# A third PSUM bank for row maxima, a respaced schedule and packed narrow products in a fused two-layer attention kernel

## The reference

```python
x = x + L0_xattn(layernorm(x), ctx)      # 16 heads of width 16, q and k normalised per head
x = x + L0_ffn(layernorm(x))             # P = x@U1 (256 -> 64), H = gelu(P@V1 + b1) (64 -> 1024),
                                         # Q = H@U2 (1024 -> 64), Q@V2 + b2 (64 -> 256)
x = x + L1_xattn(layernorm(x), ctx, mask)# one head of width 16: q = x@Wq+bq, k = c@Wk+bk, v = c@Wv+bv;
                                         # scores normalised over the keys (mean, std), softmax, @v,
                                         # the head tiled 16 times, @Wout + bout
x = x + L1_ffn(layernorm(x))             # soft mixture: logits x@phi, softmax over the batch (dispatch)
                                         # and over the slots (combine), 64 experts of 32 slots
```

## Time and profile before

| | before |
|---|---|
| median of three runs | 6526.37 us |
| the profiled execution's own time | 6520.53 us |
| its span | 6518.7 us |
| PE busy | 5927.6 us, 91% |
| DVE busy | 3677.9 us, 56% |
| ACT busy | 3300.6 us, 51% |
| POOL busy | 2407.3 us, 37% |

### The profile page before, as it was taken

One profiled execution on the slowest core, in us unless ns is written; L12 is line 12 of the kernel. 1 busy time (PEld: TensorE's weight loads), 2 busy tenths in 40 slices (PEclk: granted clock), 3 DMA queues, 4 the chain that ended last, 5 costly groups with the idle time before them and its releaser, 6 DMA issues. The chain is left out here.

```text
span 6518.7 us, 93097 instructions
## 1 busy us (share of the span) xinstructions
PE 5927.6 (91%) x35613; PEld 2981.1 (46%) x35613; DVE 3677.9 (56%) x6989; ACT 3300.6 (51%) x6257; POOL 2407.3 (37%) x2686
## 2 busy tenths in 40 slices
PE   3789999999999999999999999997599999998999
PEld 1223333333333333333333333322388888886888
DVE  3565656656566565565665656661366666652333
ACT  1366666666666666666666666654222222223332
POOL 3226355363462634636346364443222222220000
PEclk9799999999999999999999999997799999999999
DMA  2441432414324143241332423310356666666553
GB/s 63 78 76 51 79 72 58 83 50 77 69 58 85 49 76 69 61 86 50 74 70 60 84 56 71 62 28 15 127 187 214 221 213 214 209 211 249 211 195 117
DMA packets 417819, 680.30 MB, mean 104 GB/s; under 512 B 61376, under 2 KB 316432, under 8 KB 415072
## 3 DMA queue, kind: packets, MB, share of 16 engines
q1 hardware_dynamic: 307552, 565.29, 34.0%
q10 hardware_dynamic: 109824, 109.07, 5.0%
HBM read 455.04 MB, written 218.39 MB: 103 GB/s over the span
## 5 line engine op out<-in xcount | busy, mean ns | idle before, releaser
L1193 DVE TENSOR_REDUCE mx<-psum 128x1 f32<-128x401 f32 x4096 | 2212.1, 570 | 1612.8 <-PE psum L767 1603.7
L1038 ACT ACTIVATE probs<-psum 128x512 f32<-128x512 f32 (+1 forms) x3328 | 1910.5, 599 | 906.6 <-PE psum L789 903.5
L767 PE MATMUL psum<-kst,qst 96*128 96x401 bf16 x4096 | 1354.9, 343 | 191.9 <-DVE mx L1193 150.9
L789 PE MATMUL psum<-qst,kst 99*128 99x512 bf16 (+1 forms) x3328 | 1284.5, 386 | 49.8 <-ACT probs L1038 44.8
L800 PE MATMUL psum<-probs,vaug 128*17 128x512 f32 x6656 | 885.8, 604 | 0.0
L789 PEld LDWEIGHTS psum<-qst,kst 99*128 99x128 bf16 (+1 forms) x3328 | 328.8, 99 | 1177.1 <-ACT probs L1038 750.4
L767 PEld LDWEIGHTS psum<-kst,qst 96*128 96x128 bf16 x4096 | 402.6, 98 | 961.4 <-DVE mx L1193 756.1
L1486 POOL TENSOR_TENSOR disp<-disp,rz 128x2048 f32<-128x2048 f32 x64 | 294.3, 4599 | 925.4 <-DVE rz L1716 925.4
L1505 PE MATMUL psum<-phi,xT 128*128 128x128 f32 x4096 | 512.2, 280 | 39.2 <-DMA xT<-xnT_scratch 31.9
L1520 PE MATMUL psum<-disp,xnb 128*128 128x128 f32 x4096 | 495.5, 280 | 49.9 <-DMA xnb<-xn_scratch 30.7
L1505 PEld LDWEIGHTS psum<-phi,xT 128*128 128x128 f32 x4096 | 480.4, 193 | 86.9 <-issue 79.2
(11 more groups left out here) (190 smaller groups left out, 7527.2 us busy)
## 6 DMA issues: line engine op xcount, KB each, us to landing
xnb<-xn_scratch SPq DMA_DIRECT2D x256, 512.0 KB, 3.8
kst<-k_planes SPq DMA_DIRECT2D x384, 200.1 KB, 8.7
logit_scratch<-disp ACTq DMA_DIRECT2D x64, 1024.0 KB, 5.3
xT<-logit_scratch SPq DMA_DIRECT2D x32, 2048.0 KB, 8.3
k_planes<-pl SPq DMA_DIRECT2D x96, 384.0 KB, 3.2
y_scratch<-ysb ACTq DMA_DIRECT2D x128, 256.0 KB, 5.3
vaug<-v_scratch SPq DMA_DIRECT2D x64, 442.0 KB, 4.3
v_scratch<-vst SPq DMA_DIRECT2D x48, 544.0 KB, 3.1
```

Source lines behind the costliest of these rows:

```text
L767: mm(to[:, 0:PW], qst[g][0:NP, j, t * P:(t + 1) * P], kst[g][0:NP, j, k0:k0 + PW], start=True, stop=True).then_inc(m_full, 1)
L789: mm(bank[S_BANK[n % 2]][0:m, :], kst[g][0:NR, j, c * P:c * P + m], qst[g][0:NR, j, :], start=True, stop=True).then_inc(s_full, 1)
L1038: fn(probs[0:m, 4 * (k % 2) + j, :], bank[S_BANK[j % 2]][0:m, :], ACT.Exp, scale=float(HD) ** 0.5).then_inc(s_exp, 1)
L1193: v.tensor_reduce(mx[:, n % 2, u // 4, u % 4:u % 4 + 1], bank[M_BANK[r % 2]][:, 0:PW], AX.X, ALU.max).then_inc(m_free, 1)
```

## The change

Four things change together.

1. The ring for pieces gets a third bank, number 7, in 43 of the 52 steps (`LENT`: all but steps 38 to 46). The ring is now a list of homes: each use takes the bank that has been free for longest.
2. The tail, which had banks 6 and 7, keeps bank 6 alone except in steps 38 to 46, where `pv1` and `out` use bank 7. What alternated between the two now waits for its predecessor's copy; `V1` 4 to 7 go to the head's bank 5.
3. The pieces of a step stand elsewhere: the second comes behind the second score product, the third behind place 1, the fourth behind place 2, and the last behind `weigh_values`. The positions of nearly all tail entries are new.
4. Narrow products are packed in the array. `kv1` is cut into four lots of 128 tokens, each into its own 32 partitions of the bank; `U2` takes two chunks at once, into partitions 0 to 63 and 64 to 127, and `v2` sums the halves by a doubled weight; `s1` takes two chunks of keys at once, one on array rows 0 to 63 and one on rows 64 to 127, into banks 5 and 6. For this the layer 1 keys and queries are kept twice in SBUF, and the mean of the keys needs one small product (`km` on PE, `sel`).

Pieces of the diff that the prediction speaks of:

```diff
-        put((11.0, 11.34, 11.67, 12.0, 15.9, 16.67, 17.67, 18.67)[f], -1, "V1", f)
+        put((11.34, 12.0, 12.67, 13.34, 16.67, 17.67, 18.36, 20.0)[f], -1, "V1", f)
...
-        put(35.0 + 0.5 * c, -1, "s1", c)
+    for p in range((KC + 1) // 2):
+        put((36.0, 37.0, 38.34, 39.34, 40.67, 41.67, 43.0)[p], -1, "s1", p)
...
+LENT = [s < 38 or s > 46 for s in range(STEPS)]
...
+    last = {2: None, 3: None, 7: None}
+    ring, homes, back = {}, [], {}
+    for i, (use, k) in enumerate(order):
+        free = [m for m in (2, 3, 7) if m != 7 or (LENT[k % STEPS] and k < B * STEPS)]
+        home = min(free, key=lambda m: -1 if last[m] is None else last[m])
+        homes.append((home, last[home]))
...
                 for k in range(2):
-                    last = mm(hb[0:2 * A1, 0:m], w1kv[:, k, :], cT[:, n % 2, k, 0:m], start=(k == 0), stop=(k == 1))
+                    for j in range(-(-m // P)):
+                        w = min(P, m - j * P)
+                        last = mm(hb[32 * j:32 * j + 32, 0:w], w1kv[:, k, :], cT[:, n % 2, k, j * P:j * P + w],
+                                  start=(k == 0), stop=(k == 1), skip_group_check=True)
...
             def ring_bank(use):
-                n = RING[use]
-                if n >= 2:
-                    pe.wait_ge(m_free, n - 1)
-                return bank[M_BANK[n % 2]]
+                home = HOMES[RING[use]]
+                if home[1] is not None:
+                    pe.wait_ge(m_free, home[1] + 1)
+                if len(home) == 3 and home[2] >= 0:
+                    pe.wait_ge(t_dve, at("t_dve", home[2], "res", 3, QT - 1))
+                return bank[home[0]]
...
             def ffn_up(b, f):
-                before = ("u1",) if f < 2 else ("V1", f - 2) if f < 5 else ("V1", f - 1)
-                pe.wait_ge(t_act, at("t_act", b, *before))
-                to = b7 if f in (1, 3) else b6
-                mm(to[:, :], v1[:, f * P:(f + 1) * P], pT[0:RANK, :], start=True, stop=True).then_inc(t_mm, 1)
+                if f < 4:
+                    pe.wait_ge(t_act, at("t_act", b, *(("V1", f - 1) if f else ("u1",))))
+                    to, signal = b6, t_mm
+                else:
+                    head_bank(b, "V1", f)
+                    to, signal = hb, h_full
+                mm(to, v1[:, f * P:(f + 1) * P], pT[0:RANK, :], start=True, stop=True).then_inc(signal, 1)
...
+            def ffn_down(b, p):
+                if p == 0:
                     pe.wait_ge(t_act, at("t_act", b, "V1", 3))
-                pe.wait_ge(g_post, at("g_post", b, "gpost", f))
-                mm(b7[0:RANK, :], u2[:, f, :], hx[:, f % 4, :], start=(f == 0), stop=(f == FC - 1)).then_inc(t_mm, 1)
+                pe.wait_ge(g_post, at("g_post", b, "gpost", 2 * p + 1))
+                for a in range(2):
+                    last = mm(b6[RANK * a:RANK * a + RANK, :], u2[:, 2 * p + a, :], hx[:, (2 * p + a) % 4, :],
+                              start=(p == 0), stop=(p == FC // 2 - 1), skip_group_check=True)
+                last.then_inc(t_mm, 1)
...
+            def layer_one_scores(b, p):
+                head_bank(b, "s1", p)
+                if p >= 1:
+                    pe.wait_ge(t_act, at("t_act", b, "s1", p - 1))
                 else:
                     pe.wait_ge(t_dve, at("t_dve", b, "q1a"))
-                mm(to[0:m, :], kv1T[:, c * P:c * P + m], q1a, start=True, stop=True).then_inc(signal, 1)
+                c, m = 2 * p, key_rows(2 * p)
+                mm(hb[0:m, :], kv1T[0:64, c * P:c * P + m], q1a[0:64, :], start=True, stop=True).then_inc(h_full, 1)
+                if c + 1 < KC:
+                    mm(b6[:, :], kv1T[64:P, (c + 1) * P:(c + 2) * P], q1a[64:P, :], start=True,
+                       stop=True).then_inc(t_mm, 1)
...
                     woven_steps(b, steps, s, 0)
-                    piece()
                     score_columns(b, g, c, 1)
                     piece()
                     woven_steps(b, steps, s, 1)
+                    piece()
                     score_columns(b, g, c, 2)
+                    woven_steps(b, steps, s, 2)
                     piece()
-                    woven_steps(b, steps, s, 2)
                     score_columns(b, g, c, 3)
-                    piece()
```

More of the change, by code:

```diff
@@ new lines, in woven @@
+        put((12.68, 13.35, 14.01, 14.68, 18.35, 19.35, 20.35, 21.35)[f], -1, "gpost", f)
+    for p in range(FC // 2):
+        put((16.34, 18.34, 21.67, 23.67)[p], -1, "U2", p)
+    put(24.34, -1, "pT2")
+    put(25.0, -1, "v2", 0)
+    put(25.34, -1, "res", 2, 0)
+    put(25.67, -1, "v2", 1)
+    put(26.34, -1, "res", 2, 1)
+    put(27.34, -1, "lnv", 2)
+    put(27.35, -1, "lna", 2)
+    put(27.36, -1, "base", 3)
+    put(29.0, -1, "xT", 2, 0)
+    put(29.67, -1, "xT", 2, 1)
+    put(30.34, -1, "q1")
@@ L243, in pieces_of, with lent_until @@
     return [(n + 1, u) for u in range(u0, u0 + PIECES[c])]
+LENT = [s < 38 or s > 46 for s in range(STEPS)]
 def ring_uses():
-    order = [("piece", 0, u) for u in range(64)] + [("max", 0)]
-    order += [("piece",) + p for k in range(-AHEAD, 0) for p in pieces_of(k)]
+    order = [(("piece", 0, u), 0) for u in range(64)] + [(("max", 0), 0)]
+    order += [(("piece",) + p, 0) for k in range(-AHEAD, 0) for p in pieces_of(k)]
     for k in range(B * STEPS):
         n, c = divmod(k, KC)
-        pieces = [("piece",) + p for p in pieces_of(k)]
+        pieces = [(("piece",) + p, k) for p in pieces_of(k)]
         order += pieces[:1]
         if c == OUT_STEP and n >= 1:
-            order.append(("out", n - 1))
+            order.append((("out", n - 1), k))
         if c == MAX_STEP and n + 1 < B * G:
-            order.append(("max", n + 1))
+            order.append((("max", n + 1), k))
         order += pieces[1:]
-    order.append(("out", B * G - 1))
-    return {use: i for i, use in enumerate(order)}
-RING = ring_uses()
+    order.append((("out", B * G - 1), B * STEPS))
+    last = {2: None, 3: None, 7: None}
[4 more added lines that the diff above has]
+        homes.append((home, last[home]))
+        if home == 7:
+            b = (k - 47) // STEPS
+            if last[7] is not None and k >= 47 and (back[7] - 47) // STEPS < b:
+                homes[i] = (home, last[home], b - 1)
+            back[7] = k
+        last[home] = i
+        ring[use] = i
+    return ring, homes, [(u, k) for u, k in order]
+RING, HOMES, RING_ORDER = ring_uses()
+def lent_until(b):
+    return max(i for i, (_, k) in enumerate(RING_ORDER) if HOMES[i][0] == 7 and k < STEPS * (b + 1) + 38)
 def layers(nc, x, ctx_in, mask, w, x3_d, xn_d, xnT_d, y_d, out):
@@ L464, in _ @@
             ]
+            for j in range(4):
+                loads.append((bkv[32 * j:32 * j + A1, :], w["L1_xattn_bk"].rearrange("(p a) -> p a", a=1)))
+                loads.append((bkv[32 * j + A1:32 * j + 32, :], w["L1_xattn_bv"].rearrange("(p a) -> p a", a=1)))
             for j in range(P // HD):
```

274 lines of the change are left out of this document (146 added, 128 removed).

## The result

The kernel after takes 6435.68 us, median of four runs (6416.01 to 6438.70), against 6526.65 us before (6522.10 to 6527.11). The ratio is 0.9856, 95% interval 0.9835 to 0.9876: faster by 91 us, where 252 were forecast, and outside the range of 6190 to 6400. The profiled execution took 6438.05 us, span 6436.0.

What follows compares the result with a forecast made beforehand. PE was taken as the bound, with about 37 us of waits in a 268.68 us batch. Per batch -11.6 - 10 + 2 + 2.5 + 1 = -16.1 us, times 16, plus 5 outside the loop and 6 for the median: 6274 us, range 6190 to 6400.

Steps and rivals of the forecast that it cites:

- first sum, of what is removed: Per batch, packed products save 11.6 us on PE; the third bank and respaced pieces save 10 us.
- What comes back: Costs in the loop's batches from `s1` exponentials, `V1` in bank 5 and POOL's norms: 2 + 2.5 + 1 us a batch.
- What hides: Key loads on SP about 1.5 us later ahead of the stacks, the tail's store, POOL's feed-forward work: hidden or holding.
- (c): Tail's norms keep POOL's 6 us while steps shrink; the transpose behind waits up to 1 us more.
- (a): Two `s1` exponentials in a row on ACT delay the score product in place 0 (steps 36, 37, 43): 2 us a batch.
- (b): `V1` 4 to 7 share bank 5 with the head and wait behind `X` and at three other places: 2.5 us.
- (d): Single bank 6: copies finish within a place or more of cover, costing nothing; 4 us if that cover goes.
- A: Rival: bank wait only changes its name, score banks take over; change 2 worth 2 us instead of 10; 6400 us; chance 0.14.
- B: Rival: `s1` row halves run one after the other, 5.2 us a batch more; 6357 us; chance 0.12.
- C: Rival: moved pieces also free score products, the paid-back 5.5 us do not appear; 6194 us; chance 0.17.
- D: Rival: feed-forward part becomes a chain through POOL and ACT, slower; 6760 us at full size; chance 0.05.
- The rule that was set against the change: Packing does not speed up emptying of PSUM: `s1`'s 3.9 us worth nothing, batch gains 12 us instead of 16, 6340 us.

Runs made afterwards that it cites:

- E6: E5 with entries moved by a third or two of a step at the other new waits (`U2`, `V1` 4, `proj` 1, `v2` 1, transposes, `s1` pairs): 6180.59 us.
- E1: Kernel after with one entry moved: group 1's stacks issued in step 38, behind the load of the transposed maxima, instead of in step 33: 6346.38 us.
- E5: E1 plus POOL's order changed: the last key norm goes behind the tail's layer norm, and `base` 3 moves to step 33: 6283.96 us.
- E4: Kernel after with the ring on two banks in all 52 steps, packing and positions unchanged: 6488.91 us.
- E7: E1 with the ring on two banks in all steps: 6442.80 us.
- E8: E1 with both products of each `s1` pair on array rows 0 to 63, so one follows the other: 6398.47 us.

## Why the prediction was wrong

**What was right.** Its first sum, of what is removed, holds. A `U2` pair costs 1.01 us (1.0 to 1.1 forecast), a `kv1` 0.58 in the mean of 16 (0.65), a full-height `v2` 0.87. Two row halves start together; timeline of after:

```profile
4337.21 0.69 PE L967 MATMUL psum<-g_a,kv1T 64*128 64x512 f32 x1
4337.22 0.69 PE L969 MATMUL psum<-g_a,kv1T 64*128 64x512 f32 x1
...
4338.27 0.39 PE L832 MATMUL psum<-qst,kst 99*128 99x512 bf16 x1
```

The pair costs 1.06 us, as forecast. The empty step was forecast at 3.03 us instead of 3.53. It takes 3.04:

```profile
4332.52 1.05 PE L843 MATMUL psum<-probs,vaug 128*17 128x512 f32 x8
4333.50 0.34 PE L810 MATMUL psum<-kst,qst 96*128 96x401 bf16 x1
...
4334.29 0.57 PE L810 MATMUL psum<-kst,qst 96*128 96x401 bf16 x2
...
4335.56 0.62 PE L843 MATMUL psum<-probs,vaug 128*17 128x512 f32 x4
```

The forecast took 11.6 + 10 = 21.6 us a batch away. E6, in which most of what came back is mended, has a batch of 247.7 us, 22.0 under before. The two agree, though E6 still has waits and also moved some entries to better places, so that this is no exact proof of each term.

**The step that failed** is "What comes back", with 5.5 us a batch, and "What hides" beside it. 17.5 came back (265.2 - 247.7, taking E6 as the batch without it). By the experiments, in this order:

- 5.7 us a batch (E1, 259.5) for the load of the maxima behind two stacks. "What hides" spoke of the stacks only as something that is issued 1.5 us later. It never asked what stands behind them in the queue. No row of the prediction shows SP, and of the DMA engines it had only the mean share of a batch, 0.32, which hides the 28 us in which they are full.
- 4.5 us (E5, 255.0) for POOL's order: 3.6 in steps 29 and 30, and 1.0 in 49 and 50, where the wait stayed and only the low clock behind it became rarer. Term (c) gave the tail's norms "up to 1 us more". It priced the 6 us of the norm, which the change does not alter, and missed that the norm of the head's keys, 4.2 us, had come ahead of it: with `lna` 2 moved from position 26.68 to 27.35 it passed `kn` 4, which stands at 26.96. The wait in step 29 is 2.88 us, and in 14 of 15 batches the clock is low behind it; E5 leaves 1.14 us.
- 7.3 us (E6, 247.7) at six smaller places. Terms (a) and (b), 2 and 2.5 us, named two of them and were about right: the exponentials behind a pair in place 0 came to 1.7 (steps 36 and 37), `V1` behind `X` to 2.3 (steps 15 to 17). Term (d), the single bank 6, was put at nothing and cost 2.2: `proj` 1 (1.2, steps 5 and 6) and `v2` 1 (1.0, steps 24 to 26) wait for the residual of their predecessor in the bank. The term reckoned with ACT's copies of 0.6 us; these two are taken out by DVE, behind its reductions of pieces. The transposes behind two norms of POOL, term (c) again, came to 0.5 in steps 29 and 30 and 1.8 in 49 and 50. Steps 32 to 35, into which entries moved, took 1.1 more. E6 moved all of these at once, so the parts are read from its steps and not tested one by one.

Left out of every term was the clock. Behind most of the waits over 1 us stands a stretch at 1.2 GHz, in sum 252 us of the loop in after, 158 in E1, 65 in E5, 37 in E6, 55 before. With 197 us more at half speed than before, at most half of that, some 100 us, is the clock's own part, and it goes when the waits go. That it is not the packing that draws the clock down follows from E4 to E7, which keep it all.

The lone tail, forecast 8 us longer, came out 3 longer (from the end of the loop to the first product of the mixture layer, 184.9 to 187.7); with 195.2 us in E1 for the same tail, this neither confirms the term nor refutes it.

**The rivals.** A, the bank wait only changes its name: its time (6400) is the nearest to the measured one, but its mechanism is not what happened, and the nearness is chance. It leant on rows 3, where ACT holds the larger share of waiting weight loads; between products, the PE rows of before have 91.3 us for DVE and 25.6 for ACT. After the change ACT's waits grew only to 32.3 us, and E7 prices the third bank at 96 us, 6 a batch, not 2. Step by step, E7 loses 11.1 us a batch against E1, close to the 10 forecast, and gains 6.1 where other waits were (29: 8.23 to 5.13; 49: 5.92 to 4.05). B, serial row halves: refuted by the two starts 0.01 us apart, against 0.97 in E8. E8 puts what they are worth at 52 us, where I reckoned 83, because in place 0 and behind waits the second half is hidden. C, the payback doesn't appear: refuted for after, though E6 comes to C's time (6194). D: between 1000 and 3800 us PE has no wait for `gpost`; in the lone tail `U2` waits for POOL in both kernels (18.4 us before, 22.4 after).

The rule that was set against the change, in the Trainium skill's page "TensorEngine Tiling (Array Packing)", section "PSUM Bottleneck", would, as the prediction applied it, have made the concurrent halves worth nothing. Measured they are worth 52 us. In steps 38 to 41 the rule does not bind; in steps 36 and 37, where both exponentials stood ahead of the spine's, it does: 0.2 us instead of 0.85.

## What to carry to other kernels

A step made shorter moves every deadline closer, so for each asynchronous feeder (a load, another engine's chain) write down when it is issued, when it lands and when it is needed, and subtract the time saved in between; here two such margins took 10 of the 17.5 us that came back, one (the stacks) at an entry that the diff does not touch, one at an order that it turned over by moving `lna` 2. Compare the order on the helper engines as carefully as that on the bound one: one swap on an engine that is 38% busy was worth some 60 us (E5, which moved `base` 3 too). Ask of every bank that loses its partner which engine empties it, and what stands ahead on that engine. And price a wait on TensorE in the middle of a full stretch above its own length, since the clock often falls behind it.

## What the runs showed of the hardware

- After a single wait of about 3 us in an otherwise full stretch, the granted clock was 0.55 for the next 3.8 us, and after 1.15 us (step 16, clock 0.72 in the next 3.7 us) `weigh_values` took 1.86 us instead of 1.05:

```profile
2154.30 1.12 PE L893 MATMUL psum<-pT,v 64*128 64x512 f32 x2 [1.15 <-ACT pl L1100]
...
2155.85 1.86 PE L843 MATMUL psum<-probs,vaug 128*17 128x512 f32 x8
```

- Two float32 products on two halves of the rows, into two banks, run wholly at once (starts 0.01 us apart, 1.06 us for both; 1.92 on the same half, E8), as two do on two column groups (1.01 us for both, 1.00 for one before).
- Transfers of 4 KB took 10 us to land behind 3.2 MB of stacks from the same issuing engine, where their median is 2.1.
- The same wait does not always bring the clock down: behind 1.85 us in step 49 it was low in 14 of 14 batches of E1, 10 of after and 5 of E5.
